# A three-layer field-interaction kernel: loads, stores and queues reordered, two sums moved, the last product in halves

## The reference, cut to what matters

```python
X0 = inputs.reshape(-1, 32, 64)
Xi = X0
pools = []
for W, b in ((W1, b1), (W2, b2), (W3, b3)):       # 128 outputs each
    Wr = W.reshape(128, 32, Xi.shape[1])
    Xi = einsum('bhd,bmd,ohm->bod', X0, Xi, Wr) + b[None, :, None]
    pools.append(Xi.sum(axis=-1))
return concatenate(pools, -1) @ fc_W.T + fc_b     # 64 x 1
```

## Time and profile before

| | before |
|---|---|
| median of 3 runs | 83.1 us |
| profiled execution, its own time | 83.07 us |
| its span, first to last instruction | 81.3 us |
| TensorE busy | 75.0 us, 92% |
| GpSimd busy | 49.6 us, 61% |
| VectorE busy | 47.4 us, 58% |
| ScalarE busy | 34.6 us, 43% |
| moved by DMA | 12.01 MB |
| granted clock of TensorE | full in all slices |

### The profile page before, as it was taken

One profiled execution on the slowest core, in us unless ns is written; L12 is line 12 of the kernel. 1 busy time (PEld: TensorE's weight loads), 2 busy tenths in 40 slices (PEclk: granted clock), 3 DMA queues, 4 the chain that ended last, 5 costly groups with the idle time before them and its releaser, 6 DMA issues.

```text
span 81.3 us, 1119 instructions
## 1 busy us (share of the span) xinstructions
PE 75.0 (92%) x367; PEld 52.0 (64%) x367; DVE 47.4 (58%) x44; ACT 34.6 (43%) x51; POOL 49.6 (61%) x49
## 2 busy tenths in 40 slices
PE   4999999699999999979999999999999999999911
PEld 1335456654327767658888888888888888877600
DVE  1056998499979999597499519962002003303581
ACT  1830983968798945973756300470300300000000
POOL 4986497999992599590099889449906006064200
PEclk9999999999999999999999999999999999999999
DMA  0898999999986525259993000000000000000000
GB/s 23 283 338 249 371 366 353 383 388 387 378 261 201 157 61 141 84 149 411 370 384 153 0 4 0 4 0 0 0 0 0 0 8 0 0 0 0 0 0 0
DMA packets 7530, 12.01 MB, mean 148 GB/s; under 512 B 836, under 2 KB 3972, under 8 KB 7268
## 3 DMA queue, kind: packets, MB, share of 16 engines
q1 hardware_dynamic: 6915, 11.16, 40.0%
q10 hardware_dynamic: 608, 0.77, 3.1%
HBM read 10.88 MB, written 1.05 MB: 147 GB/s over the span
## 4 chain that ended last, share of the span: by engine, by line
PE 75%; ACT 8%; DMA 7%; DVE 4%; issue 2%; ACTq 2%; SPq 1%; DVEq 0%
PE a_ps L576 27%; PE x_ps L576 24%; DMA w_sb<-w 7%; PE z_ps L570 7%; PE a_ps L661 5%; ACT feat L357 4%; PE a_ps L634 3%; PE x_ps L596 2%; PE a_ps L623 2%; PE a_ps L622 2%; ACTq L429 2%; DVE w_sb L511 1%; DVE total L549 1%; ACT zz L357 1%; DVE x L501 1%
## 5 line engine op out<-in xcount | busy, mean ns | idle before, releaser
L265 POOL TENSOR_TENSOR feat<-r_in,feat 128x1024 fp32r<-128x1024 f32 x8 | 19.2, 2403 | 3.8 <-ACT feat L357 3.2
L576 PE MATMUL x_ps<-feat,w_hi 128*128 128x512 f32 x64 | 18.9, 395 | 0.2 <-ACT feat L357 0.2
L501 DVE SCALAR_TENSOR_TENSOR x<-a_ps,vec,x 128x512 f32<-128x512 f32 x8 | 6.0, 751 | 19.8 <-PE a_ps L623 19.7
L258 POOL TENSOR_TENSOR xs<-x_in,xs 32x512 fp32r<-32x512 f32 x7 | 11.1, 1585 | 8.8 <-ACT xs L357 8.4
L576 PE MATMUL a_ps<-feat,a_hi 128*128 128x512 f32 x64 | 16.2, 396 | 0.0
L272 POOL TENSOR_TENSOR x<-x 128x512 f32<-128x512 f32 x6 | 7.8, 1292 | 11.5 <-DVE x L501 11.3
L576 PEld LDWEIGHTS x_ps<-feat,w_hi 128*128 128x128 f32 x64 | 11.9, 188 | 3.2 <-issue 0.6
L576 PEld LDWEIGHTS a_ps<-feat,a_hi 128*128 128x128 f32 x64 | 11.9, 188 | 2.7
L481 DVE TENSOR_TENSOR feat<-z_ps,feat 128x1024 fp32r<-128x1024 f32 x8 | 9.8, 1219 | 2.2 <-ACT feat L357 2.2
L357 ACT ACTIVATE feat<-z_ps 128x1024 fp32r<-128x1024 f32 x8 | 8.2, 1021 | 6.0 <-DVE z_ps L474 5.1
L371 ACT ACTIVATE x<-x_ps,vec 128x512 f32<-128x512 f32 x8 | 5.4, 685 | 12.3 <-PE x_ps L596 12.3
(11 more groups left out here) (74 smaller groups left out, 75.7 us busy)
## 6 DMA issues: line engine op xcount, KB each, us to landing
w_sb<-w SPq DMA_DIRECT2D x9, 512.0 KB, 8.5
x_in<-xl SPq DMA_DIRECT2D x8, 256.0 KB, 7.2
r_in<-xr SPq DMA_DIRECT2D x2, 1024.0 KB, 6.2
a_by_fields<-at_sb SPq DMA_DIRECT2D x8, 96.0 KB, 2.0
x<-x ACTq DMA_DIRECT2D x1, 512.0 KB, 4.6
x<-x SPq DMA_DIRECT2D x1, 512.0 KB, 5.7
w_sb<-w SPq DMA_DIRECT2D x1, 256.0 KB, 11.1
a_by_fields<-at_sb SPq DMA_DIRECT2D x4, 64.0 KB, 1.9
```

Source lines behind the costliest of these rows:

```text
L258: nc.gpsimd.tensor_tensor(xs[rows, c, :], x_in[rows, c % X_BUFS, :], xs[rows, c, :].bitcast(f32), ALU.subtract).then_inc(xs_lo, 1)
L265: nc.gpsimd.tensor_tensor(feat[:, c, 1, of_half(1), :], z_of(c, 1), feat[:, c, 0, of_half(1), :].bitcast(f32), ALU.subtract).then_inc(lo_d ...
L501: nc.vector.scalar_tensor_tensor(out=x1[:, c, :], in0=a_ps[:, c % 2, :], scalar=vec[:, 3:4], in1=x1[:, c, :], op0=ALU.add, op1=ALU.mult).t ...
L576: nc.tensor.matmul(bank, weights[:, k, :], feat[:, c, part, k, :], start=(start and k == 0), stop=False)
```

## The change

- x16 is loaded by SP behind all of W2; then W1's rest, x of chunks 4 and 5. x of 6 goes behind A's stores, x of 7 and the second use of x16 before the right factors.
- A's stores become eight: the first two rounds in one store each, the rows H of rounds 2 and 3 in one that ACT issues (its own DMA issue of x16 at the start is gone).
- W1's main sum goes from VectorE to GpSimd, which does it before split_x(1). z16's product on GpSimd goes from the start to behind split_x(4), z16_lo behind W1's rest, both before lo(2); lo(4) waits for f_sum.
- V's banks are parts of x1_ps[1]; x1_hi(1, 0) waits for V's copies. TensorE's list between keep_clock and x1's product 3 is a new mixture.
- ACT: split_x(4) after hi(3, 0), z16_hi after save_a(2), save_zz(0) after split_x(5), hi(4, ·) behind f2's four DMA issues and save_zz(1).
- VectorE: mult(0, 1) and lo(0) before W1's low part; rest_lo before chunk 4.
- Product 7 in two halves of 256 columns; instead of reducing it, TensorE sums its eight groups of 64 columns with ones.
- keep_clock 14 and 12 become 11 and 9. `store_a` gets the engine, the wait and a count of rounds.

```diff
-        vt_ps = a_ps[:, 0, 0:M]
-        v_ps = a_ps[:, 1, 0:P]
+        vt_ps = x1_ps[1][:, 0:M]
+        v_ps = x1_ps[1][:, M:M + P]
...
+        def store_a(engine, rows, g, t, rounds, left):
+            engine.wait_ge(a_saved, t + rounds)
+            engine.dma_start(bass.AP(scratch.tensor, (left + FIELDS * t) * M, [[EXT * M, rows], [1, rounds * FIELDS * M]]),
+                             at_sb[64 * g:64 * g + rows, t:t + rounds, :]).then_inc(a_out, 16)
... SP
-            load_w2(0)
-            load_w2(1)
+            for t in range(ROUNDS):
+                load_w2(t)
+            sp.dma_start(x16[:, :, :], bass.AP(x.tensor, 0, [[N, P], [HALF * COLS, 2], [1, N]])).then_inc(x16_in, 16)
+            sp.dma_start(w1_sb[:, :, EVEN:, :], w1[:, :, EVEN:, :]).then_inc(w1_rest_in, 16)
             load_x(4)
-            load_w2(2)
-            load_w2(3)
-            sp.dma_start(w1_sb[:, :, EVEN:, :], w1[:, :, EVEN:, :]).then_inc(w1_rest_in, 16)
             load_x(5)
+            store_a(sp, EXT, 0, 0, 2, 0)
+            store_a(sp, EXT, 1, 0, 2, HALF)
+            store_a(sp, H, 0, 0, 2, H)
+            for t in range(2, ROUNDS):
+                store_a(sp, EXT, 0, t, 1, 0)
+                store_a(sp, EXT, 1, t, 1, HALF)
             load_x(6)
-            for t in range(ROUNDS):
-                sp.wait_ge(a_saved, t + 1)
-                store_a(EXT, 0, t, 0)
-                store_a(EXT, 1, t, HALF)
-                store_a(H, 0, t, H)
... GpSimd
-            nc.gpsimd.tensor_tensor(x16[:, 0, :], x16[:, 0, :], x16[:, 1, :], ALU.mult).then_inc(z16_done, 1)
+            pool.wait_ge(w1_in, 16)
+            nc.gpsimd.tensor_tensor(w1_sb[:, 0, 0:TILES, :], w1_sb[:, 0, 0:TILES, :], w1_sb[:, 1, 0:TILES, :],
+                                    ALU.add).then_inc(w_sum, 1)
...
             split_x(4)
+            pool.wait_ge(x16_in, 16)
             pool.wait_ge(xs_lo, 5)
-            lo(2)
+            nc.gpsimd.tensor_tensor(x16[:, 0, :], x16[:, 0, :], x16[:, 1, :], ALU.mult).then_inc(z16_done, 1)
             pool.wait_ge(w1_rest_in, 16)
             nc.gpsimd.tensor_tensor(w1_sb[:, 0, EVEN:, :], w1_sb[:, 0, EVEN:, :], w1_sb[:, 1, EVEN:, :],
                                     ALU.add).then_inc(w_sum, 1)
+            pool.wait_ge(z16_done, 1)
+            pool.wait_ge(hi16_done, 1)
+            nc.gpsimd.tensor_tensor(z16_lo[:, :], x16[:, 0, :], z16_hi[:, :].bitcast(f32),
+                                    ALU.subtract).then_inc(lo16_done, 1)
+            lo(2)
...
             split_x(5)
             lo(3)
+            pool.wait_ge(f_sum, 1)
             lo(4)
             lo(5)
... ACT
             hi(3, 0)
+            split_x(4)
             save_a(2)
+            act.wait_ge(z16_done, 1)
+            copy(z16_hi[:, :], x16[:, 0, :]).then_inc(hi16_done, 1)
             save_a(3)
+            store_a(act, H, 0, 2, 2, H)
             hi(3, 1)
             act.wait_ge(w_sum, 2)
             copy(w1_hi[:, EVEN:, :], w1_sb[:, 0, EVEN:, :]).then_inc(w_hi_done, 1)
             split_x(5)
-            hi(4, 0)
-            hi(4, 1)
+            save_zz(0)
             save_x1(0)
             save_x1(1)
...
+            save_zz(1)
+            hi(4, 0)
+            hi(4, 1)
+            save_x1(2)
             hi(5, 0)
             hi(5, 1)
-            save_zz(1)
... VectorE
-            mult(4, 0)
-            mult(4, 1)
             dve.wait_ge(w_hi_done, 2)
             rest_lo(w1_sb[:, 0, :, :], w1_hi, w_lo_done)
-            lo(4)
+            chunk(4)
             chunk(5)
...
+            for half in range(HALVES):
+                cols = slice(half * N // 2, (half + 1) * N // 2)
+                nc.vector.scalar_tensor_tensor(out=x1[:, CHUNKS - 1, cols], in0=a_ps[:, (CHUNKS - 1) % 2, cols],
+                                               scalar=vec[:, 3:4], in1=x1[:, CHUNKS - 1, cols], op0=ALU.add,
+                                               op1=ALU.mult).then_inc(last_done, 1)
... TensorE, the new list from the first pick of chunk 1 (the old one is L672 to L704)
+            pick_right(1, 0); pick_right(1, 1); x1_lo(0, 0); v_part(0); x1_hi(0, 1); v_part(1)
+            pick_right(2, 0); v_part(2); x1_lo(0, 1); pick_right(2, 1); v_part(3); transpose
+            pick_right(3, 0); a_round(0); a_round(1); x1_hi(1, 0); x1_lo(1, 0); pick_right(3, 1)
+            a_round(2); x1_hi(1, 1); a_round(3); x1_lo(1, 1); pick_right(4, 0); spread16(0)
+            pick_right(4, 1); x1_tail(0); x1_tail(1); spread16(1); x1_hi(2, 0); x1_lo(2, 0)
+            pick_right(5, 0); x1_hi(2, 1); x1_lo(2, 1); pick_right(5, 1); x1_tail(2); x1_product(3)
...
+            nc.tensor.matmul(y_ps, ones[:, :], total[:, :], start=False, stop=False)
+            for d in range(N // B):
+                if d % (N // B // HALVES) == 0:
+                    pe.wait_ge(last_done, d // (N // B // HALVES) + 1)
+                last = nc.tensor.matmul(y_ps, ones[:, :], x1[:, CHUNKS - 1, d * B:(d + 1) * B],
+                                        start=False, stop=(d == N // B - 1))
```

More of the change, by code:

```diff
@@ L302, in _ @@
             nc.gpsimd.tensor_scalar(b23[:, :], vec[:, 1:3], float(D), 0.0, ALU.mult, ALU.add).then_inc(b23_done, 1)
-            pool.wait_ge(x16_in, 16)
-            nc.gpsimd.tensor_tensor(x16[:, 0, :], x16[:, 0, :], x16[:, 1, :], ALU.mult).then_inc(z16_done, 1)
-            pool.wait_ge(z16_done, 1)
+            pool.wait_ge(w1_in, 16)
+            nc.gpsimd.tensor_tensor(w1_sb[:, 0, 0:TILES, :], w1_sb[:, 0, 0:TILES, :], w1_sb[:, 1, 0:TILES, :],
+                                    ALU.add).then_inc(w_sum, 1)
+            pool.wait_ge(w_sum, 1)
+            pool.wait_ge(xs_lo, 1)
             split_x(1)
-            pool.wait_ge(hi16_done, 1)
             pool.wait_ge(xs_lo, 2)
-            nc.gpsimd.tensor_tensor(z16_lo[:, :], x16[:, 0, :], z16_hi[:, :].bitcast(f32),
-                                    ALU.subtract).then_inc(lo16_done, 1)
-            pool.wait_ge(lo16_done, 1)
             split_x(2)
@@ L387, in _ @@
             split_x(0)
+            split_x(1)
             act.wait_ge(w_sum, 1)
             copy(w1_hi[:, 0:TILES, :], w1_sb[:, 0, 0:TILES, :]).then_inc(w_hi_done, 1)
-            split_x(1)
-            act.wait_ge(z16_done, 1)
-            copy(z16_hi[:, :], x16[:, 0, :]).then_inc(hi16_done, 1)
             hi(0, 0)
@@ L395, in _ @@
             split_x(2)
-            save_zz(0)
             hi(1, 0)
@@ L408, in _ @@
             hi(2, 0)
-            split_x(4)
             hi(2, 1)
@@ L446, in _ @@
             copy(q_sb[:, :], q_ps).then_inc(q_saved, 1)
+            split_x(6)
             hi(6, 0)
@@ L579, in x1_hi @@
             def x1_hi(c, half):
+                if c == 1 and half == 0:
+                    pe.wait_ge(v_saved, 3)
                 if c >= 2 and half == 0:
@@ L669, in _ @@
             pick_right(0, 1)
-            keep_clock(12)
+            keep_clock(9)
             x1_hi(0, 0)
@@ L673, in _ @@
             pick_right(1, 1)
-            spread16(0)
             x1_lo(0, 0)
             v_part(0)
+            x1_hi(0, 1)
             v_part(1)
+            pick_right(2, 0)
             v_part(2)
-            pick_right(2, 0)
+            x1_lo(0, 1)
+            pick_right(2, 1)
             v_part(3)
-            pick_right(2, 1)
             pe.wait_ge(ident_done, 2)
@@ L684, in _ @@
             nc.tensor.transpose(v_ps, vt_sb[:, :], ident[:, :]).then_inc(v_ready, 1)
-            x1_hi(0, 1)
+            pick_right(3, 0)
             a_round(0)
-            pick_right(3, 0)
             a_round(1)
+            x1_hi(1, 0)
+            x1_lo(1, 0)
             pick_right(3, 1)
             a_round(2)
+            x1_hi(1, 1)
             a_round(3)
+            x1_lo(1, 1)
             pick_right(4, 0)
-            x1_lo(0, 1)
+            spread16(0)
             pick_right(4, 1)
[L695 to L699, removed]
             x1_tail(0)
             x1_tail(1)
+            spread16(1)
+            x1_hi(2, 0)
+            x1_lo(2, 0)
+            pick_right(5, 0)
+            x1_hi(2, 1)
+            x1_lo(2, 1)
             pick_right(5, 1)
-            spread16(1)
-            x1_product(2)
+            x1_tail(2)
             x1_product(3)
@@ L728, in _ @@
             pe.wait_ge(ones_done, 1)
-            for i in range(2):
-                pe.wait_ge(total_done, i + 1)
-                last = nc.tensor.matmul(y_ps, ones[:, :], total[:, i, :], start=False, stop=(i == 1))
+            pe.wait_ge(total_done, 1)
+            nc.tensor.matmul(y_ps, ones[:, :], total[:, :], start=False, stop=False)
[4 more added lines that the diff above has]
+                                        start=False, stop=(d == N // B - 1))
             last.then_inc(y_ready, 1)
```

48 lines of the change are left out of this document (20 added, 28 removed).

## The result

The changed kernel takes 87.73 us as the median of four runs (87.24 to 88.98), the one before 83.10: 1.054 times as long, 95% interval 1.047 to 1.060. The median is over all four; the ratio leaves out the one of 88.98 us, whose clock was granted at 0.977 where the others had 1.00. Forecast were 86.2 us, between 83.5 and 87.8. The profiled execution took 88.08 us for a span of 86.3.

What follows compares the result with a forecast made beforehand. TensorE was taken to bound the kernel, so the start of A's product for chunk 0 decides: 83.07 + 3.5 for its later start - 0.35 at the end = 86.2 us; own range 85.6 to 87.2, wide range 83.5 to 87.8.

Steps and rivals of the forecast that it cites:

- the three stalls: TensorE waits before spread16(0), 2.1 us; before pick_right(5, 1), 0.9 to 1.0; before product 4's last low part, 1.35.
- slow f_sum: Rival: VectorE's sum f_sum meets other traffic and takes 2.73 us, not 1.20; + 1.5, 87.7 us; chance 0.05.
- The load that all hangs on: Chunk 4's x, now issued behind W2, the pairs' x and W1's rest, lands at 23.6 us; bounds 22.65 and 24.3.
- What is queued behind it: Chain over ACT and GpSimd behind chunk 4's x: z16_lo 5.4 us after its landing, chunk 0's tail ends 8.05 after.
- From the tails to A's product: From the end of chunk 0's tail to A's product for chunk 0: 13.5 us, start at 45.2, 3.5 later than before.
- The first 27 us: Front up to pick_right(4, 0): ends at 26.9 to 27.2 us, 1.6 to 1.9 later, with 2.3 us more work done.
- rival 1: Chunk 4's x comes early, so hi(3, 0) at 22.65 us sets the chain; time 85.2 us; chance 0.14.
- The end: Last product in halves, summed by TensorE: y ready at about 79.1 for 79.46 us, gain 0.35; bounds 0.6 and -0.2.
- Eight stores for twelve: Fewer stores of A: worth nothing, since they land before ACT, which comes later, asks for them.
- That TensorE stays the bound: Rival: TensorE bounds the whole changed kernel, A's product starts at 39.6, time 80.6 us; chance 0.14.
- The clock falls in one of the new waits: Rival: TensorE's clock drops in a new wait of about 2 us, costing up to 2.7; 87 to 88.9 us; chance 0.04.

Runs made afterwards that it cites:

- the kernel with all three gone: Changed kernel with more blank matmuls, no wait for f_sum before lo(4), chunk 4's first half early, its x loaded and rounded where it was: 84.25 us.
- three of these on the old order: Kernel before with the last product in halves summed by TensorE, V in x1's bank, second zz copied before chunk 5's rounding: 81.25 us, ratio 0.978.

## Why the prediction was right, point by point

**The size was short, and that it stayed in the range is in part luck.** Direction, path and place of the three stalls came as forecast, but the median of 87.73 lies above the forecast's own range of 85.6 to 87.2 and 0.07 us under the end of the wide one, 87.8. That end was set for a slow f_sum, which did not come. In the profiled execution A's product started at 47.23 for 45.2: 1.0 us of it is the landing, 0.8 the way to the tail of chunk 0, 0.2 the rest. The end gave 0.17 back: 86.2 + 2.0 - 0.17 = 88.0, for 88.08.

**The load that all hangs on: right, and 1 us short.** It landed at 24.6 in the profiled execution, 23.6 was taken by counting bytes. The count was right, the pace was not, for two reasons. With one queue the second and third slice moved 250 and 248 GB/s where two queues had moved 283 and 338. By single landings, the third quarter of W2 was in at 18.8 to 19.6 us in the five profiles of this order with one queue, with 5.0 MiB through; with x16 on ACT's queue again 5.5 MiB were through at 19.5 and the load landed at 23.8. The other reason is scatter: in each of the 13 profiles one load between 18 and 25 us lands later than its bytes account for, by 0.2 to 1.6 us, by 1.5 in the profile of the changed kernel and by 0.2 in that with more blanks, whose load landed at 23.3. What this pause is stays open. Chunk 1's x gained 1.1 us from the 0.5 MB no longer ahead of it, chunk 2's only 0.5. That completion need not follow the order of issue (the Trainium skill, DMA: Bandwidth & Descriptors, Queues, rings and completion order) did not help the load: here it landed 0.65 us behind W1's rest, the last one ahead of it, and in all 13 profiles these loads landed in their order.

**What is queued behind it: right in every link, 0.8 us short at the end.** I had z16_lo ready 5.4 us behind the start of the chain; it was 5.6, and the first pause 2.2 us for 2.1. The tail of chunk 0 ended 8.85 us behind (33.46) for 8.05: I gave rest_lo 1.0 us from the earlier trace rows and said it wasn't last; it took 1.72 beside GpSimd's lo(2), and ended 0.33 behind zz, which had been forecast as the last. It ended 0.28 us behind lo(2) itself:

```profile
30.16 2.40 POOL L268 TENSOR_TENSOR feat<-r_in,feat 128x1024 fp32r<-128x1024 f32 x1
...
31.12 1.72 DVE L505 TENSOR_TENSOR w_hi<-w_sb,w_hi 32x256 fp32r<-32x256 f32 x1 [4.86 <-ACT w_hi L367]
```

Its 1.0 us in the kernel before was no length of its own either: there it ended 0.28 us behind GpSimd's split, which had started before it.

**From the tails to A's product: right.** Second pause 1.17 us for 0.95, third 0.97 for 1.35. The third was smaller because f_sum took 0.68 us, not the 1.20 that I took from W1's sum. W1's sum had GpSimd's product of the pairs beside it at its start, so it was no measure of a sum alone. In all A's product came 22.6 us behind the landing, for 21.6. The two pauses are worth 0.72 and 1.41 us by the profiles of the runs that remove them, 2.1 for the 2.3 of the sum.

**The first 27 us: too quick by about one microsecond.** pick_right(4, 0) ended at 28.1 for 26.9 to 27.2. In the profiled execution it cost nothing, as TensorE waited behind it anyway. But hi(3, 0), forecast to end at 22.65, ended at 23.90, with the front as late. So a load landed at 23.6, as forecast, would have been rounded from 23.9 only, and rival 1's 22.65 was out of reach in this execution.

**The end: right, 0.52 for 0.35**, and shown to be the part's own.

**Eight stores for twelve are worth nothing:** not tried alone. ACT asked for A's stores after their landing, as far as the trace shows it.

**Rivals.** That the load comes early: no. That TensorE stays the bound: no; the two later pauses, which I had called independent of the load, cost 0.7 and 1.4 us by themselves, and the kernel with all three gone still needs 84.25. That f_sum is slow again: no, the reverse, as long as GpSimd waits for it. **The clock falls in one of the new waits: this I undervalued.** I gave it 0.04 and looked for it at the later pauses. It does happen in one of four executions of the changed kernel (88.98 us, 0.977). The two profiles that caught it, of the runs with chunk 4's x loaded earlier, have it from 12 us on, behind the two early pauses near 9 and 11 us and not at the later ones. It costs: in the first of these kernels 89.05 to 89.43 against 87.41 us. The blank matmuls at the start, which I read as 1.2 GHz, start 0.43 us apart, but the granted clock in the profile is 1.00 there, so this view doesn't bear the reading out. The Trainium skill (TensorE: Matmul & The Clock Gate, Part 1) says that idling brings the half clock back; these two traces agree, 0.50 to 0.57 from 12 to 15 us behind a stretch in which TensorE was busy for 1.4 and 1.3 of 3 us. But the profile with x16 on ACT's queue had it busy for only 0.87 of the same 3 us, with pauses of 1.12 and 1.13, and kept 1.00. And the kernel before was recorded with a mean of 0.987 to 0.990 in eight of 30 executions, without loss (83.09 to 83.20 us); where its clock dipped no profile shows. Why one execution falls and the next does not stays open here.

## What to carry to other kernels

When one engine is the bound and nearly without gaps, price a reordering by walking every other engine's list from the latest load that stands in it: here one late 256 KB load stood in front of a chain over GpSimd and ACT. It was not all: putting it and its rounding back won 1.2 to 2.0 of the 4.6 us, and two waits further down the lists, which don't depend on it, 0.7 and 1.4. Take the parts of such a change apart and keep those that remove a wait of the bounding engine; three of these on the old order gave 2.2%, where the whole gave -5.4%. A pause of the matmul engine early in the kernel is not free even where later work would absorb it, because the clock may fall behind it, which took 1.6 to 2.0 us here.

## What the runs showed of the hardware that I had not expected

- An fp32 sum of 128x512 on VectorE, both inputs in SBUF, took 0.68 us while GpSimd stood still (seven profiles) and 2.73 to 2.76 us beside GpSimd's subtraction (six profiles). Where GpSimd's instruction had started first, the sum ended 0.55 us behind its end in all six, as if it had waited for it whole. W1's low rest, 32x256, took 0.61, 0.99 or 1.72 us and ended 0.28 us behind GpSimd's instruction each time. So such a duration read from a trace holds only for what ran beside it.

```profile
42.84 0.68 DVE L533 TENSOR_TENSOR f<-f 128x512 f32<-128x512 f32 x1
```

The kernel before, beside GpSimd:

```profile
34.34 2.38 POOL L265 TENSOR_TENSOR feat<-r_in,feat 128x1024 fp32r<-128x1024 f32 x1 [0.88 <-ACT feat L357]
...
34.53 2.73 DVE L528 TENSOR_TENSOR f<-f 128x512 f32<-128x512 f32 x1
```

- Taking 0.5 MB out of the way of the first loads saved chunk 2's x 0.5 us and not the 1.4 that its bytes took at the later pace, as one queue started slower than two.
- In the orders with two pauses of 0.4 to 1.1 us close together (or one of 1.17) the clock fell in nine of 22 executions; with six blank matmuls in the pauses it fell in none of 16.
